# Both ends of a sixteen-head attention pipeline reordered, with a split key row, a later x load and fewer filler matmuls

## The chip, the core and the metric

The kernel runs on one core of a Trainium2 chip. The metric is the device time of that core in microseconds, lower is better. TensorE (PE) multiplies, VectorE (DVE) and ScalarE (ACT) empty the accumulator banks, GpSimd (POOL) does small vector work and indirect DMAs, SyncE (SP) issues most of the loads and stores. The engines run separate instruction streams, which meet only at semaphores.

## The reference, cut to what matters

Four layers of a decoder, each a gated cross attention on a context and a gated feed-forward block, on x of 8 batches x 256 tokens x 256 features. The context has 120 rows for each batch. Every block reads the layer norm of x.

```python
x = x + tanh(g[0]) * attn0(ln(x), ctx)   # one head of 256, key mask
x = x + tanh(f[0]) * moe0(ln(x))         # 8 experts pick 256 tokens each, plus a shared one
x = x + tanh(g[1]) * attn1(ln(x), ctx)   # 16 heads of 16, key bias and mask
x = x + tanh(f[1]) * fourier(ln(x))      # one 256 x 256 matrix after folding
x = x + tanh(g[2]) * attn2(ln(x), ctx)   # 16 heads of 16, key mask
x = x + tanh(f[2]) * ternary(ln(x))      # 256 -> 1024 -> gelu, layer norm -> 256
x = x + tanh(g[3]) * attn3(ctx, ctx, ln(x))  # one head of 256
x = x + tanh(f[3]) * moe3(ln(x))         # top-1 routing, 8 experts of 256 slots
```

Softmax of a one-head attention adds one number for each key to the scores (the mask and the bias terms folded through the weights): the *key row*, 960 numbers for the 8 batches.

## The kernel before

The order on each engine is written out by hand, and one function for each small job stands on each engine with matching semaphores.

**Start.** The two weight matrices of the one-head attention are turned (`turn_weights`), copied by ACT and multiplied (`product`), so that keys come straight from the context. `column` makes two bias columns, `key_row` multiplies one of them (`wkb`) with the context, ACT's `take_row` and a DVE instruction make `krow` of it. `fill(bank, n)` issues n matmuls of ones whose result nobody reads. Each appears in the trace as two instructions. There are fills of 15, 4 and 12 around this work.

**The one-head layers** (`one_gate(L)`, L = 0 and 3) run over 8 batches k. In step s PE turns the normalised rows (`turn_z`), turns the probabilities of the batch before (`turn_p`), makes keys and values of the next (`keys_values`), the scores (`scores`), and for the batch two back the router's turn and logits (`gate_turn`, `logits`) after the product with the values. `scores` first adds the key row to all rows by a float32 matmul with one row of ones. DVE takes the maximum (L1647), ACT the exponential (L1360). For L = 3 the router also finds a slot for each token (`pick_expert`, `group_ranks`, `find_slots` in four groups), POOL moves each of the 16 tiles of rows to its slots by an indirect DMA (`move`), and SP loads the sorted rows `G3` back (L400) for the experts. `FILL` and `fill` calls pad PE here; the last two are 40 before the moves have landed and 22 after.

**The sixteen-head pipeline** (`stream`) runs over 16 units v = 8 batches x layers 1 and 2 in steps s = 0 to 17. Unit v has its scores in step v, turned scores, exponentials and half of its product with the values in step v + 1, and the rest, the normalising and the output product in step v + 2; side work (the Fourier block, and the layer norm of the ternary block) follows in steps from 3 on. Accumulator bank 6 is shared by turned z, queries, keys, values and the side turns; each of them waits for the copy out of the one before it. Banks 0 to 3 hold the scores, 4 and 5 the product with the values, 7 the maxima and outputs. `browT` holds the additive key rows of layers 1 and 2 as three bfloat16 parts, for three rows of ones in `scores`. `tern_rows` makes, ahead of the first step, a row of weights (banks 4 and 5) and two rows of sums (bank 7) for the ternary block. After the last step come 16 tiles of the ternary block (`tern_hidden`, `tern_turn`, `tern_out` on PE; `gelu`, `take_high` on ACT; `tern_stats` L2081, `tern_low` L2088, `tern_add` on DVE; `weigh` L561 on POOL).

Of the kernel before, what the change touches and what calls it, by code (L numbers as in the profile page):

```python
# [5 lines left out]
ALU = mybir.AluOpType  # L6
# [7 lines left out]
P = 128  # L14
# [14 lines left out]
FILL = {0: {0: 6}, 3: {5: 8, 6: 14, 7: 18}}  # L29
# [27 lines left out]
def flamingo_kernel(nc, d, out):  # L57
    ctx = ExitStack()
    with ctx:
# [141 lines left out]

        c.at = 18906
# [73 lines left out]
        UN = 2 * NB  # L276
        one = sems("one", f"{ln_names} K_ps KT_sb V_sb s_ps nmax p_sb pT_ps pT_sb y_ps x")
# [14 lines left out]
        def _(sp):  # L292
# [3 lines left out]
            sp.dma_start(W["v0"][:, :, :], d["Wv0"]).then_inc(load["values"], 16)  # L296
            sp.dma_start(x[:, 4:, :], d["x"][:, 4:, :]).then_inc(load["x"], 16)
# [111 lines left out]
        def _(g):  # L409
# [130 lines left out]
            def stream():  # L540
# [75 lines left out]
        def _(pe):  # L616
# [40 lines left out]
            fill(psum[7], 15)  # L657
# [32 lines left out]
            def one_gate(L):  # L690
# [26 lines left out]
                def scores(k):  # L717
                    pe.wait_ge(q["KT_sb"], b0 + k + 1)
                    pe.wait_ge(q["zT_sb"], b0 + k + 1)
                    if k >= 1:  # L720
                        pe.wait_ge(q["p_sb"], b0 + k)
                    else:
                        pe.wait_ge(su["krow"], 1 + L // 3)
                    o = psum[3][:, 0:TB * SK].rearrange("p (t n) -> p t n", t=TB)
                    mm(o, onesf[0:1, :], bcast(krow[0:1, k * SK:(k + 1) * SK], 1, TB), True, False)
# [49 lines left out]
                def group_ranks(n):  # L775
# [5 lines left out]
                    if n == 3:  # L781
                        fill(psum[3], 12)
# [8 lines left out]
                def main():  # L791
                    pe.wait_ge(su["B_sb"], 1 if L == 0 else 3)
                    if L == 0:
                        fill(psum[7], 12)
# [32 lines left out]
                    else:  # L827
# [3 lines left out]
                        fill(psum[3], 22)  # L831
# [167 lines left out]
            pe.wait_ge(su["col_sb"], 2)  # L999
# [5 lines left out]
            def stream():  # L1005
# [5 lines left out]
                def turn_z(v):  # L1011
# [3 lines left out]
                    else:  # L1015
                        pe.wait_ge(q["V_sb"], max(v, 1))
# [17 lines left out]
                def keys(v):  # L1034
                    L, k = layer(v)
                    if 1 <= v < 5:
                        pe.wait_ge(q["q_sb"], v + 1)
# [4 lines left out]
                    for m_ in range(KC):  # L1042
                        for c in range(KC):
                            m = mm(psum[6][:, m_ * SK:(m_ + 1) * SK], W[f"k{L}"][:, c, m_ * P:(m_ + 1) * P],
# [3 lines left out]
                def values(v):  # L1048
# [7 lines left out]
                    for c in range(KC):  # L1056
                        m = mm(psum[6][0:SK, 0:D], ctxT[:, c, k * SK:(k + 1) * SK], W[f"v{L}"][:, c, :], c == 0, c == KC - 1)
# [1175 lines left out]
```

## Time and profile before

| what | value |
|---|---|
| median of three runs | 892.33 us (891.32 to 895.99) |
| the profiled execution | 897.07 us, its span 895.3 us |
| PE matmul busy | 855.6 us, 96% |
| DVE, ACT, POOL busy | 461.7, 326.6, 210.3 us |
| mean granted TensorE clock | 0.987 |

The profile shows one execution. Times of instructions are microseconds from the start of the span. A group's row gives the start of its first instruction, the time to the end of its last, engine, source line, operation and tiles, and in brackets the idle time before it with what ended it. PEld is the weight load of TensorE. Matmuls are pipelined, so that a PE that is busy all the time need not be at its peak. The 1.8 us between 897.07 and 895.3 lie outside the span.

### The profile page before, as it was taken

To read this page: it belongs to the slowest core of one execution; us is meant where nothing else is said; L and a number is where in the kernel's file an instruction comes from. 1 tells how busy PE (TensorE), PEld (TensorE's weight loads), DVE (VectorE), ACT (ScalarE), POOL (GpSimd) and SP (SyncE) were. 2 spreads that over 40 slices of the span, in tenths; PEclk is the share of its full clock that TensorE was granted. 3 is DMA by queue.
4 is the path that set the end of the run, shared out by engine and by line. 5 is a ranking of instruction groups with operands and counts; after the bars stand their busy time and mean duration, and the time that the engine had idled before them with its cause. 6 is when DMAs were issued, how large, how long until landed. Compare 5 with 4: busy or idle time off the path is not lost.

```text
span 895.3 us, 15721 instructions
## 1 busy us (share of the span) xinstructions
PE 855.6 (96%) x6100; PEld 669.5 (75%) x6108; DVE 461.7 (52%) x1240; ACT 326.6 (36%) x628; POOL 210.3 (23%) x241
## 2 busy tenths in 40 slices
PE   8999999999999998889999999988999999999997
PEld 7776665678888876667777777755777779988886
DVE  2773676500132306577777777766998786000000
ACT  2434122112322222555555645646554441112121
POOL 1121233020434310000100101114665116112212
PEclk9997999999999999899999999999999999999999
DMA  7031911014746338000000000000000012336451
GB/s 238 25 130 36 303 76 50 25 53 165 231 156 198 112 95 300 1 2 1 2 2 1 2 1 1 2 1 1 2 1 2 30 42 91 125 115 201 146 167 22
DMA packets 33877, 70.64 MB, mean 79 GB/s; under 512 B 9218, under 2 KB 23946, under 8 KB 28939
## 3 DMA queue, kind: packets, MB, share of 16 engines
q1 hardware_dynamic: 26937, 59.92, 18.8%
q0 software_dynamic: 6144, 8.31, 4.8%
q10 hardware_dynamic: 722, 1.39, 0.4%
q8 instruction: 49, 0.80, 0.4%
q14 instruction: 25, 0.20, 0.1%
HBM read 54.98 MB, written 14.80 MB: 78 GB/s over the span
## 4 chain that ended last, share of the span: by engine, by line
PE 88%; DVE 6%; ACT 3%; issue 2%; DVEq 1%; POOL 0%; POOLq 0%; ACTq 0%
PE banks L618 80%; DVE small L2018 2%; PE banks L1127 2%; PE banks L1206 1%; ACT arena L1308 1%; PE banks L954 1%; PE banks L1141 1%; ACT arena L1360 1%; PE banks L714 1%; PE banks L1020 1%; ACT arena L1489 1%; PE banks L1165 1%; ACT arena L1504 0%; DVE arena L2058 0%; DVE small L1647 0%
## 5 line engine op out<-in xcount | busy, mean ns | idle before, releaser
L618 PE MATMUL banks<-arena 32*120 32x256 f32 (+6 forms) x1808 | 160.1, 378 | 7.2 <-DVE small L2018 4.2
L1308 ACT ACTIVATE arena<-banks 128x512 f32<-128x512 f32 (+4 forms) x185 | 106.8, 597 | 163.1 <-PE banks L1091 34.3
L618 PEld LDWEIGHTS banks<-arena 32*120 32x120 f32 (+5 forms) x1808 | 99.6, 164 | 38.4 <-issue 19.0
L618 PE MATMUL banks<-ffw,arena 128*128 128x256 bf16 (+2 forms) x632 | 116.7, 338 | 0.5 <-issue 0.2
L618 PE MATMUL banks<-arena,ew 128*128 128x256 f32 x512 | 113.3, 379 | 1.4 <-ACT arena L1308 1.4
L618 PE MATMUL banks<-ew,arena 128*128 128x256 f32 x512 | 113.2, 379 | 0.0
L618 PEld LDWEIGHTS banks<-arena,ew 128*128 128x128 f32 x512 | 97.1, 190 | 15.0 <-ACT arena L1308 1.8
L618 PEld LDWEIGHTS banks<-ew,arena 128*128 128x128 f32 x512 | 96.2, 190 | 12.5
L618 PEld LDWEIGHTS banks<-ffw,arena 128*128 128x128 f16 (+1 forms) x640 | 84.5, 135 | 23.8 <-issue 2.4
L2018 DVE TENSOR_REDUCE small<-banks 128x16 f32<-128x1920 f32 x32 | 69.1, 2158 | 23.6 <-PE banks L618 23.6
L1965 DVE TENSOR_SCALAR arena<-banks,arena 128x256 f32<-128x256 f32 x16 | 7.1, 479 | 120.7 <-PE banks L618 120.7
L1504 ACT ACTIVATE arena<-banks,mcol 120x2048 f32<-120x2048 f32 x32 | 63.2, 1974 | 16.6 <-PE banks L618 16.6
L545 POOL TENSOR_TENSOR small<-small,mhalf 128x2 f32<-128x2 f32 x16 | 11.1, 694 | 210.9 <-DVE small L1989 210.9
L618 PE MATMUL banks<-arena,ffw 128*128 128x512 f32 x128 | 60.4, 615 | 0.0
L1445 ACT ACTIVATE arena<-banks,b1T 128x256 f32<-128x256 f32 x64 | 26.9, 471 | 77.8 <-PE banks L618 77.8
L1942 DVE TENSOR_SCALAR small<-arena,tg 128x2 f32<-128x2 f32 x8 | 1.8, 228 | 97.0 <-PE banks L618 97.0
L1447 ACT ACTIVATE arena<-banks 128x256 f32<-128x256 f32 x64 | 21.1, 381 | 83.2 <-PE banks L618 83.2
L1338 ACT ACTIVATE arena<-banks,b1T 128x512 f32<-128x512 f32 x32 | 21.9, 687 | 76.9 <-PE banks L618 76.9
L430 POOL TENSOR_TENSOR small<-small,mhalf 128x2 f32<-128x2 f32 x31 | 22.6, 730 | 107.4 <-DVE small L1624 107.4
L506 POOL DMA_INDIRECT out<-arena x14 | 21.8, 1557 | 92.5 <-DVE arena L1965 64.8
L516 POOL DMA_INDIRECT arena<-zrow,small x16 | 17.9, 1116 | 103.4 <-DVE arena L1947 57.0
L618 PEld LDWEIGHTS banks<-arena,ffw 128*128 128x128 f32 x128 | 23.4, 195 | 23.1 <-issue 22.6
(244 smaller groups left out, 1309.8 us busy)
## 6 DMA issues: line engine op xcount, KB each, us to landing
ew<-in_w SPq DMA_DIRECT2D x32, 1024.0 KB, 7.2
xrow<-arena SPq DMA_DIRECT2D x1, 2064.0 KB, 20.9
arena<-xrow SPq DMA_DIRECT2D x8, 258.0 KB, 4.3
zrow<-arena SPq DMA_DIRECT2D x8, 256.0 KB, 2.2
ffw<-in_shared SPq DMA_DIRECT2D x2, 1024.0 KB, 6.4
acc<-x SPq DMA_DIRECT2D x4, 512.0 KB, 3.5
ffw<-in_tern SPq DMA_DIRECT2D x2, 1024.0 KB, 8.2
out<-x SPq DMA_DIRECT2D x8, 256.0 KB, 2.0
```

Source lines behind the costliest of these rows:

```text
L430: g.tensor_tensor(rstd[:, 2 * a:2 * a + 2], ve[:, 2 * a:2 * a + 2], mhalf[:, 0:2], ALU.pow).then_inc(q["rstd"], 1)
L506: g.indirect_dma_start(to, bass.IndirectOffsetOnAxis(ap=at(e, j), axis=0), eout[:, e % 2, j, :], None, compute_op=ALU.add, **kw).then_inc( ...
L516: g.indirect_dma_start(G[:, u, j, 0:ROW], None, zrow, bass.IndirectOffsetOnAxis(ap=idx[:, TB * e + j:TB * e + j + 1], axis=0))\
L545: g.tensor_tensor(rstd[:, 2 * u:2 * u + 2], ve[:, 2 * u:2 * u + 2], mhalf[:, 0:2], ALU.pow)\
L618: return pe.matmul(o, l, r, start=a, stop=b)
L1127: m = pe.transpose(OW[:, 512 * t + g_ * P:512 * t + (g_ + 1) * P], OP[:, g_, t * P:(t + 1) * P], ident[:, :])
L1308: return nc.scalar.activation(o, i_, ACT.Copy)
L1338: nc.scalar.activation(hT[:, m_, :], psum[m_ % 4][:, :], ACT.Gelu_apprx_tanh, bias=b1T[:, E * MC + m_:E * MC + m_ + 1]).then_inc(sh["h_sb" ...
L1445: m = nc.scalar.activation(heT[:, u, m_, :], src, ACT.Gelu_apprx_tanh, bias=b1T[:, n * MC + m_:n * MC + m_ + 1])
L1447: m = nc.scalar.activation(heT[:, u, m_, :], src, ACT.Relu)
L1504: nc.scalar.activation(PT[0:SK, c].rearrange("p h n -> p (h n)"), SC[0:SK, :], ACT.Exp, bias=mcol[0:SK, L - 1, k:k + 1]).then_inc(q["p_exp ...
L2018: V.tensor_reduce(nmx[:, t, :], s, AX.X, ALU.max, negate=True).then_inc(q["max"], 1)
```

## The change

1. **Start.** The fills are 8, 2 and none (from 15, 4, 12). The column for `wkb` is made first, in bank 7, and handed over with a semaphore of its own. ACT issues the context's load after the two tiny ones, and SP issues the rest of x only when the context has landed.
2. **First steps of the stream.** `tern_rows` is split in three, put between `keys(0)`, `values(0)`, `turn_z(0)` and `queries(0)`. DVE normalises batch 0 ahead of `take_values(0)`. Unit 1 has its keys and values in bank 5; in step 0 its keys come ahead of the second half of the scores and its queries behind it, and its values are made in step 1. ACT and DVE take them in the same order.
3. **Steps 2 and 3** issue `output(s - 2)` ahead of `values(s + 1)`.
4. **End of the stream.** `side_norm(14)` moves from step 17 to behind `tern_stats(2)`; `tern_stats(0)` goes ahead of the last `add_output`, `tern_low(0)` ahead of `tern_stats(1)`.
5. **Key row of layer 3.** POOL splits `krow` into three bfloat16 parts in steps 8 to 10 (`key_part`), SP copies each into a row of `browT`, and `scores` of L = 3 uses one bfloat16 matmul with three rows of ones.
6. **Fills in layer 3**: `FILL` 8, 14, 18 becomes 6, 14, 15; 12 becomes 9 in `group_ranks`; 22 becomes 5 after the moves.

```diff
-FILL = {0: {0: 6}, 3: {5: 8, 6: 14, 7: 18}}
+FILL = {0: {0: 6}, 3: {5: 6, 6: 14, 7: 15}}
...
+        def kv(v):
+            return 5 if v == 1 else 6
...
             sp.dma_start(W["v0"][:, :, :], d["Wv0"]).then_inc(load["values"], 16)
+            sp.wait_ge(load["ctx"], 16)
             sp.dma_start(x[:, 4:, :], d["x"][:, 4:, :]).then_inc(load["x"], 16)
...
+            for p in range(3):
+                sp.wait_ge(su["parts"], p + 2)
+                sp.dma_start(browT[p:p + 1, 0, :], kpart[0:1, :]).then_inc(load["parts"], 16)
...
+                def key_part(p):
+                    if p == 0:
+                        g.wait_ge(su["krow"], 2)
+                        g.wait_ge(multi["s_ps"], 2 * NB)
+                    else:
+                        g.wait_ge(load["parts"], 16 * (p + 1))
+                    g.tensor_copy(kpart[0:1, :], krow[0:1, :])
+                    g.drain().then_inc(su["parts"], 1)
+                    if p < 2:
+                        g.tensor_tensor(krow[0:1, :], krow[0:1, :], kpart[0:1, :], ALU.subtract)
+                        g.drain()
...
+                    if NB <= s < NB + 3:
+                        key_part(s - NB)
+                    elif s == NB + 3:
+                        g.wait_ge(load["parts"], 16 * 4)
...
-            fill(psum[7], 15)
+            fill(psum[7], 8)
...
-            fill(psum[7], 4)
+            fill(psum[7], 2)
             pe.wait_ge(su["wT_sb"], 2)
             pe.wait_ge(load["cols"], 16)
+            column(psum[7][:, 0:KC], WT[:, 1], COL["q0"]).then_inc(su["col_ps"], 1)
             product(psum[4], WT[:, 1], WT[:, 0]).then_inc(su["B_ps"], 1)
             column(psum[5][:, 0:KC], WT[:, 0], COL["k0"])
-            column(psum[5][:, KC:2 * KC], WT[:, 1], COL["q0"])
...
-                    mm(o, onesf[0:1, :], bcast(krow[0:1, k * SK:(k + 1) * SK], 1, TB), True, False)
+                    if L == 0:
+                        mm(o, onesf[0:1, :], bcast(krow[0:1, k * SK:(k + 1) * SK], 1, TB), True, False)
+                    else:
+                        mm(o, ones[0:3, :], bcast(browT[0:3, 0, k * SK:(k + 1) * SK], 1, TB), True, False)
...
-                        fill(psum[3], 12)
+                        fill(psum[3], 9)
...
                     if L == 0:
-                        fill(psum[7], 12)
                         pe.wait_ge(load["values"], 32)
...
                         fill(psum[3], 40)
                         pe.wait_ge(gt["moved"], 16 * NT)
-                        fill(psum[3], 22)
+                        fill(psum[3], 5)
...
                 keys(0)
+                tern_weights()
                 values(0)
-                tern_rows()
+                tern_row(0)
                 turn_z(0)
+                tern_row(1).then_inc(su["trow_ps"], 1)
...
+                    if s == 1:
+                        values(1)
                     if past:
                         attend(s - 2, 1)
-                    if free and new:
+                    if new and (free or s == 0):
                         keys(s + 1)
...
                     if now:
                         scores(s, 1)
-                    if spectrum:
+                    if spectrum or s == 0:
                         queries(s + 1)
...
-                    if new:
+                    if past and not free:
+                        output(s - 2)
+                    if new and s:
                         values(s + 1)
-                    if past:
+                    if free:
                         output(s - 2)
...
             act.dma_start(cols[:, :], d["cols"]).then_inc(load["cols"], 16)
-            act.dma_start(ctxT[:, :, :], d["ctxT"]).then_inc(load["ctx"], 16)
             act.dma_start(tg[:, :], d["g"].partition_broadcast(P)).then_inc(load["tiny"], 16)
             act.dma_start(m0_i[0:1, :], d["m0"]).then_inc(load["tiny"], 16)
+            act.dma_start(ctxT[:, :, :], d["ctxT"]).then_inc(load["ctx"], 16)
...
                         first_stats()
+                        v.wait_ge(su["col_ps"], 1)
+                        V.tensor_copy(wkb, psum[7][:, 0:KC]).then_inc(su["col_sb"], 1)
                         first_rows()
-                        v.wait_ge(su["col_ps"], 1)
-                        V.tensor_copy(wkb, psum[5][:, KC:2 * KC])
+                        v.wait_ge(su["col_ps"], 2)
...
+                v.wait_ge(load["x0"], 32)
+                norm_batch(0)
+                norm_batch_end(0)
                 take_values(0)
-                v.wait_ge(load["x0"], 32)
-                for n in range(2):
-                    norm_batch(n)
-                    norm_batch_end(n)
+                norm_batch(1)
+                norm_batch_end(1)
...
-                    if s >= 3:
+                    if 3 <= s <= UN:
                         side_norm(s - 3)
-                    if s + 1 < UN:
+                    if 1 <= s < UN - 1:
                         take_values(s + 1)
+                    if s == UN + 1:
+                        tern_stats(0)
                     if s >= 2:
                         add_output(s - 2)
-                tern_stats(0)
+                tern_low(0)
                 tern_stats(1)
-                tern_low(0)
+                tern_low(1)
                 tern_stats(2)
-                tern_low(1)
+                side_norm(UN - 2)
```

## Rows read from the trace of the kernel before

**Rows 1.** The page's part 4: the chain that ended last, by engine.

```profile
PE 88%; DVE 6%; ACT 3%; issue 2%; DVEq 1%; POOL 0%; POOLq 0%; ACTq 0%
```

**Rows 2.** Windows: length, busy time (instructions) of PE, PEld, DVE, ACT, POOL, PEclk, DMA share, GB/s.

```profile
1.40:4.40 3.00, 2.98 (x14) 2.98 (x15) 0.00 (x0) 0.66 (x1) 0.28 (x1) 1.00 0.73 214
...
66.00:68.00 2.00, 2.00 (x7) 1.40 (x8) 0.75 (x3) 0.00 (x0) 0.69 (x1) 0.50 0.00 0
...
356.00:360.00 4.00, 2.81 (x26) 1.78 (x22) 3.02 (x6) 2.27 (x3) 0.00 (x0) 0.50 0.00 0
```

**Rows 3.** Timeline of the start.

```profile
1.42 4.96 PE L618 MATMUL banks<-onesf 128*128 128x128 f32 x30 [1.42 <-POOLq L414]
...
3.34 0.37 ACTq L1326 DMA_DIRECT2D rows<-in_rows  x1
...
5.21 0.37 DVE L1780 TENSOR_REDUCE small<-ident 128x16 f32<-128x128 f32 x1 [5.21 <-DMA ident<-in_ident]
...
6.23 0.60 PE L630 MATMUL banks<-ident,Wq 128*128 128x128 f32 x4
...
12.31 0.99 PE L618 MATMUL banks<-ctxT,small 128*1 128x240 f32 x16 [0.47 <-DVE cols L1722]
...
13.23 2.94 PE L618 MATMUL banks<-onesf 128*128 128x128 f32 x24
...
23.13 0.74 DVE L1619 BATCH_NORM_STATS2 small<-x 128x6 f32<-128x256 f32 x2
```

**Rows 4.** DMA issues of the first 30 us: queue, KB each, microseconds to landing.

```profile
x<-in_x SPq DMA_DIRECT2D x1, 1536.0 KB, 12.1
ctxT<-in_ctxT ACTq DMA_DIRECT2D x1, 960.0 KB, 7.2
...
rows<-in_rows ACTq DMA_DIRECT2D x1, 128.0 KB, 11.6
```

**Rows 5.** Timeline of the stream's first steps.

```profile
338.17 3.66 PE L618 MATMUL banks<-ffw,small 128*128 128x256 bf16 x32
...
345.94 0.38 PE L618 MATMUL banks<-browT,ones 3*128 3x480 bf16 x4 [0.93 <-ACT arena L1478]
...
356.93 2.16 DVE L2018 TENSOR_REDUCE small<-banks 128x16 f32<-128x1920 f32 x1 [0.81 <-PE banks L618]
...
368.96 1.97 ACT L1504 ACTIVATE arena<-banks,mcol 120x2048 f32<-120x2048 f32 x1 [1.09 <-PE banks L618]
```

**Rows 6.** Timeline of step 2: the values of unit 3.

```profile
384.64 1.12 PE L618 MATMUL banks<-Wv,ctxT 128*120 128x256 f32 x4 [0.77 <-ACT arena L1489]
```

**Rows 7.** Timeline of the stream's last step and the first ternary tiles.

```profile
616.55 4.00 POOL L561 TENSOR_TENSOR arena<-arena 128x1024 f32<-128x1024 f32 x2 [1.02 <-ACT arena L1531]
616.77 3.93 DVE L2058 TENSOR_SCALAR arena<-x,small,arena 128x256 f32<-128x256 f32 x2
...
624.98 1.16 PE L1206 MATMUL banks<-ident,arena 128*128 128x128 f32 x8 [1.79 <-DVE arena L2088]
```

**Rows 8.** Timeline of layer 3, step 3: the key row and the scores.

```profile
717.78 0.67 PE L618 MATMUL banks<-krow,onesf 1*128 1x240 f32 x2
...
718.38 1.15 PE L618 MATMUL banks<-arena 128*128 128x120 f32 x8
```

**Rows 9.** The chain in order of time, layer 3: start, length, what.

```profile
709.09 3.45 PE banks L618 x22
...
716.10 3.45 PE banks L618 x22
```

**Rows 10.** Timeline from the last router work to the first expert.

```profile
759.57 14.09 PE L618 MATMUL banks<-onesf 128*128 128x128 f32 x124
...
767.30 3.97 SPq L400 DMA_DIRECT2D arena<-xrow  x8
773.39 0.47 PEld L954 LDWEIGHTS banks<-ident,arena 128*128 128x128 f32 x4
```

**Rows 11.** The line L400: the loads of the sorted rows.

```profile
DMA to landing us min/median/max: 2.8/4.3/5.1
```

More of the change, by code:

```diff
@@ L200, in flamingo_kernel @@
         digit = c.take(2 * P, "p (a t e) -> p a t e", dt=F16, a=2, e=E)
+        c.at = 15360
+        kpart = c.take(NB * SK, dt=BF16)
         c.at = 18906
@@ L721, in scores @@
                         pe.wait_ge(q["p_sb"], b0 + k)
+                    elif L == 0:
+                        pe.wait_ge(su["krow"], 1)
                     else:
-                        pe.wait_ge(su["krow"], 1 + L // 3)
+                        pe.wait_ge(load["parts"], 16 * 4)
                     o = psum[3][:, 0:TB * SK].rearrange("p (t n) -> p t n", t=TB)
-                    mm(o, onesf[0:1, :], bcast(krow[0:1, k * SK:(k + 1) * SK], 1, TB), True, False)
+                    if L == 0:
+                        mm(o, onesf[0:1, :], bcast(krow[0:1, k * SK:(k + 1) * SK], 1, TB), True, False)
+                    else:
+                        mm(o, ones[0:3, :], bcast(browT[0:3, 0, k * SK:(k + 1) * SK], 1, TB), True, False)
                     for t in range(TB):
@@ L998, in _ @@
             pe.wait_ge(su["B_sb"], 3)
-            pe.wait_ge(su["col_sb"], 2)
+            pe.wait_ge(su["col_sb"], 3)
             pe.wait_ge(sh["x"], T // 512 * 2 + 1)
@@ L1182, in tern_rows, with tern_row @@
                            ident[:, :], True, True)
-                    for a in range(2):
-                        for m_ in range(MC):
-                            for l in range(2):
-                                m = mm(psum[7][:, a * D:(a + 1) * D], lnhl[:, l, a, m_:m_ + 1].to_broadcast([P, P]), wp[:, m_, :],
-                                       m_ == 0 and l == 0, m_ == MC - 1 and l == 1)
-                    m.then_inc(su["trow_ps"], 1)
+                def tern_row(a):
+                    for m_ in range(MC):
+                        for l in range(2):
+                            m = mm(psum[7][:, a * D:(a + 1) * D], lnhl[:, l, a, m_:m_ + 1].to_broadcast([P, P]), wp[:, m_, :],
+                                   m_ == 0 and l == 0, m_ == MC - 1 and l == 1)
+                    return m
                 def tern_hidden(t):
@@ L1248, in stream @@
                         turned_scores(s - 1, 0)
-                    if new and not free:
+                    if 1 <= s < 4:
                         queries(s + 1)
@@ L1488, in take_keys @@
                         for e in range(2):
-                            m = nc.scalar.activation(KB[:, v % 3, c, e], psum[6][:, c * SK:(c + 1) * SK], ACT.Identity,
+                            m = nc.scalar.activation(KB[:, v % 3, c, e], psum[kv(v)][:, c * SK:(c + 1) * SK], ACT.Identity,
                                                      bias=kb[:, L - 1, c, e:e + 1], scale=par[:, e:e + 1])
@@ L1542, in stream @@
                 act.wait_ge(ex["y_sb"], E)
-                for part in (take_keys, take_z, take_queries):
-                    part(0)
+                take_keys(0)
+                take_z(0)
                 act.wait_ge(su["trow_ps"], 1)
@@ L1547, in stream @@
                     copy(wrow[:, 512 * j:512 * (j + 1)], psum[4 + j])
+                take_queries(0)
                 for s in range(UN + 2):
@@ L1558, in stream @@
                         take_O(s - 2)
-                    if free and new:
+                    if new and (free or s == 0):
                         take_keys(s + 1)
@@ L1573, in stream @@
                         take_back(s - 2)
-                    if new and not free:
+                    if 1 <= s < 4:
                         take_keys(s + 1)
@@ L2103, in stream @@
                         maxima(s, 0)
+                    if s == 1:
+                        take_values(1)
                     if s >= UN - 1:
```

18 lines of the change are left out of this document (9 added, 9 removed).

## The prediction

> **What bounds the kernel now.** I read the chain that ended last first: TensorE carries 88% of it [rows 1]. So what counts is TensorE's idle time, the work that it does for nothing, and its clock. The windows show the clock twice at 0.50, its 1.2 GHz level, in a stage with regular short waits and in the first steps of the stream [rows 2]. Then I read the timelines of the places that the edits touch and looked, for each, at what TensorE waits for last. In the middle of the stream and in the experts it is busy without pause; no edit touches these. The sum is made against the profiled execution's 897.07 us; the median of the runs shown, 892.33, is 4.7 below it, and the forecast is taken from the median.
>
> **1. Start.** The 15 fills end at 1.42 + 4.96 = 6.38, and the transposes begin at 6.23, overlapping their tail [rows 3]. The identity that they need has landed at 5.21, and Wq stands ahead of it in the same queue [rows 3]. The first 14 fill instructions take 3.0 us, 0.213 each [rows 2], the later fills 2.94 / 24 = 0.12 [rows 3]. So 8 fills (16 instructions) end near 4.7, and the transposes start at 5.3: 0.9 gained. From there to the key row it is 6.1 us of work, in which the order of the columns changes nothing in sum; the 4 fills that become 2 lie under ACT's copy. The key row waited 0.47 for DVE's column [rows 3]; that column is now ready first, 0.47 gained. The key row ends at 13.3 and 12 fills follow up to 16.17 [rows 3]; without them the first keys could start at 12.0 where they started at 16.0. They also need the value row of 128 KB, issued last in ACT's queue at 3.34 and landed 11.6 later, at 14.9 [rows 3, 4]. That row shared the DMA with the 1536 KB of x, which took 12.1 us [rows 4]. Now x starts only when the context is in. The context took 7.2 us; issued 1.1 later with less beside it I put it, and the row behind it, at 9 to 10.5. So the term is 4.0, of which I take **3.8**. Its lower end is 1.0 (the row still lands at 14.9), its upper end 4.2. SP's queue behind its new wait holds the rest of x and fourteen further loads; the first to be missed is x. It is wanted by DVE for the third batch at 23.13 [rows 3], now 19.3. Loaded from 9.5 with a share of the queue, it comes at 15 to 17; if it takes 12.1 as before, it comes 2.3 late, and that is the price of that cover.
>
> **2. First steps of the stream.** Before, TensorE does the weight row and then 3.66 us of sums [rows 5] in one piece, after it turns z, waits for ACT's copy, and makes the queries. Now the weight row (some 1.7) fills the wait for the first key copy, and the second half of the sums (1.8) covers ACT's copy of z (1.2 with its wait). DVE and the reload of x give back about 1: the normalised batch 0 is wanted 3 us earlier than before and is not ready. Net 1.7: the first scores move from 345.94 [rows 5] to 344.3. In step 0 the queries of unit 1 (2.0) no longer stand between the first maximum and the second half of the scores, which waited 1.0 too long for them: 2.7. The next scores waited for a chain of queries, keys, copy (1.5) and values (1.1); the keys now come early in their own bank and the values later, so what is left is the queries and their copy: 3.4 to 3.7, and DVE's maximum of unit 1 moves from 356.93 [rows 5] to 353.2. From there on the work of step 1 ran at clock 0.50 [rows 2]: the turned scores took about 1.1 longer than in the next pair, the maxima waited with them. With TensorE fed more densely I take the clock as kept, 1.3 more: the exponential of 368.96 [rows 5] comes at 364.0. Term **5.0**, lower end 3.5 (the clock falls here all the same), upper end 5.7. ACT's copies of the weight row (1.1) now precede the query copy; they are covered by the queries' own 2.0.
>
> **3. Steps 2 and 3.** TensorE waits 0.77 for ACT's key copy before the values [rows 6], while the output product, whose input is ready, stands behind. Swapped, it fills that wait: 0.77 in each of two steps, **1.5**. Lower end 0 (ACT's exponential, which ends about 0.2 before the next scores can start, becomes the bound), upper end 1.6.
>
> **4. End of the stream.** DVE's two normalising instructions take 3.93 us, from 616.77 to 620.70, exactly under POOL's pair of 4.00 [rows 7]; elsewhere in the stream such a pair takes 0.73. All of DVE's work behind them is late: the copies that TensorE's second tile turn waits 1.79 for, until 624.98 [rows 7]. With `side_norm(14)` moved and the low part of tile 0 first, that low part is there at 622.9. TensorE then goes on when its own hidden product ends, at 623.0: 2.0 gained. Moved behind the third tile's statistics, `side_norm(14)` (0.73, or up to 2.0 more under the next POOL instruction) makes the first `tern_add` late, for which TensorE's second output product waits: 0.4 lost. Term **1.6**, from 0.5 to 2.2.
>
> **5. Key row in three parts.** The float32 key row starts at 717.78 and the scores behind it at 718.38 [rows 8]: 0.60. The nearest row for the new form is the stream's: four bfloat16 matmuls of 480 columns in 0.38 [rows 5], with the next matmul some 0.2 after their start. So one of 240 columns is 0.2, and 0.4 is saved in each batch. The chain runs through this block with period 7.01 (716.10 - 709.09) [rows 9]. DVE has 0.8 idle in such a step, so it does not stop a saving of 0.4. From the router's first group on (steps 6 and 7) DVE has no idle time, and nothing is gained. Six batches, **2.4**, from 1.0 to 3.0. The price is five POOL instructions on one partition and three DMAs, in three steps of the stream in which POOL is idle for most of the time. Queued behind them on POOL is the side layer norm's power, wanted by DVE some 5 us later. A POOL instruction of 1024 columns took 2.0 [rows 7], so copy and subtraction cost up to 4.0 of these 5: nothing.
>
> **6. Fills of layer 3.** The fills of 8 and 18 in the router steps end about when their input is there, so 2 and 3 fewer gain 0.4 once. After the router 124 instructions run in 14.09 [rows 10], 0.114 each: 40 fills end at 768.7, the last 22 at 773.5, and then the first expert turns its rows at 773.39. These rows are issued at 767.30 [rows 10] and land 2.8 to 5.1 later [rows 11], the first of them, I take it, with the least: 770.1. With 5 fills TensorE is free at 769.8. Term 3.2 with the start of the fills unchanged against the moves, taken as **3.0**; if the first load lands with the median, 4.3, it is 1.8. The moves themselves start with the router's slots, which move with term 5.
>
> **Sum.** 3.8 + 5.0 + 1.5 + 1.6 + 2.4 + 3.0 = 17.3. Against the profiled execution 897.07 - 17.3 = 879.8; from the median 892.33 - 17.3 = **875.0**. The lower ends add to 7.8 (884.5), the upper ends (3.3 for the last) to 20.0 (872.3).
>
> **The clock weighed.** The profiled execution has two stretches at 0.50 and is 4.7 above the median, so I price a further stretch at 3 to 5. Removed fills leave TensorE idle for 0.6 at the start and 0.3 before the experts. The Trainium skill, in TensorE: Matmul & The Clock Gate, section HAM oscillation, has TensorE fall back to half rate when it idles and return only after sustained work, which speaks against removing fills. By it the start would run slow again; by the rows TensorE is past its slow level from about 4.4 us on, and the idle stretches are far shorter than the regular waits of a layer-0 step, which it ran through at 1.00 for 40 us.
>
> **The rivals.**
> - *The clock falls once more than before*, at the start (6.1 us of work at 0.213 to 0.12: up to 4.5 lost) or in layer 3 with its thinner fills. For it: regular short waits did bring it down at 66 [rows 2]. Against it: 105 of the 151 fills stay. 875.0 + 4.5 = 879.5. Chance 0.17.
> - *Gains that other waits take over*: the value row lands late (2.8 less), the first sorted rows with the median (1.2), the key row is hidden under DVE (2.4). 875.0 + 6.4 = 881.4. Chance 0.14.
> - *POOL's split stalls DVE.* Rows 7 show two DVE instructions held for as long as POOL's run. Five instructions of up to 2.0 in steps 8 to 10 could hold DVE 10 us; about half of it would reach TensorE, which is busy all through these steps: 880. The Trainium skill, SBUF — State Buffer, section Who interferes with whom, makes this an exclusive lock between GpSimd and a DVE instruction of this kind; the trace agrees with its 3.93 beside 4.00. Chance 0.05.
> - *The clock does not fall in layer 0 either*, since its steps are 3.8 earlier: 871. Chance 0.07.
> - *Slower: POOL holds up the side chain.* `key_part` waits on POOL for the DMA of the part before; the side power is behind it, then DVE's side work, then TensorE's side turn in bank 6. It decides when copy, landing and subtraction take over 10 us in each of steps 8 to 11: 17.3 are used up by 4.4 lost in each, and 5.7 lost makes 898. Against it: small loads of the sorted rows landed in 2.8 [rows 11]. Chance 0.03.
> - *It does nothing that can be measured*: 890. Chance 0.03.
>
> **Numbers.** The forecast itself has 0.51, with a range of its own of 871.5 to 878.5. 868 to 884 takes in the first five cases. A measurement of this kernel tells 0.5%, 4.5 us, from no change. Faster 0.94, within it 0.03, slower 0.03.
>
> **What would show it.** Right: the transposes at 5.3, the first keys near 12, no clock of 0.50 between 340 and 365, the exponential of unit 0's second half 4.9 nearer to the stream's first keys, no DVE pair of 3.9 at the end, a layer-3 period of 6.6, and the first expert 2.8 to 3.2 after the sorted rows' issue. Wrong: first keys at 15, steps 8 to 10 longer than the 17.05 of their neighbours, or a new stretch at 0.50 in a place with fewer fills.

## The result, and the profile after

| | kernel before | changed kernel |
|---|---|---|
| beside each other, four executions each | 892.3 us (891.32 to 895.99) | 881.28 us (881.06 to 882.34) |
| the profiled execution | 897.07 us | 881.06 us, its span 879.3 us |
| on another chip, 11 and 5 executions | 899.21 us (896.45 to 903.04) | 883.55 us (882.79 to 884.82) |

The ratio is 0.9864, 95% interval 0.9832 to 0.9897; on the second chip 0.983, 0.9805 to 0.9855. So the change makes the kernel faster, inside the wide range of the forecast (868 to 884) but outside the forecast's own 871.5 to 878.5: by 11.0 us between the medians where 17.3 were forecast. On the second chip the medians differ by 15.7, profile against profile it is 16.0.

The same instructions in the two traces show where it comes from. Each pair is the start of one instruction, in microseconds:

| landmark | before | after | gained so far |
|---|---|---|---|
| first weight turns | 6.23 | 4.99 | 1.24 |
| key row of layer 0 | 12.31 | 10.93 | 1.38 |
| first keys of layer 0 | 16.01 | 11.84 | 4.17 |
| first keys of the stream | 332.75 | 323.15 | 9.60 |
| exponential of unit 0's second half | 368.96 | 353.49 | 15.47 |
| second ternary tile's turn | 624.98 | 606.12 | 18.86 |
| side turn of unit 14 | 636.42 | 621.43 | 14.99 |
| a key row of layer 3, early | 703.25 | 687.47 | 15.78 |
| the next one | 710.77 | 696.62 | 14.15 |
| the fills of 40 | 759.57 | 743.61 | 15.96 |
| issue of the sorted rows | 767.30 | 753.05 | 14.25 |
| first expert of layer 3 | 773.39 | 755.87 | 17.52 |
| end of the span | 895.3 | 879.3 | 16.0 |

Four gains are given back: 3.9 us behind the second ternary turn, 1.6 between two key rows, 1.7 between the fills of 40 and the issue of the sorted rows, 1.5 in the first expert. The start, in the timeline, answers to [rows 3]:

```profile
1.42 3.78 PE L646 MATMUL banks<-onesf 128*128 128x128 f32 x16 [1.42 <-POOLq L425]
...
3.18 0.45 ACTq L1365 DMA_DIRECT2D rows<-in_rows  x1
4.99 1.06 PE L658 MATMUL banks<-ident,Wq 128*128 128x128 f32 x4
...
10.89 0.33 SPq L305 DMA_DIRECT2D x<-in_x  x1
10.93 0.98 PE L646 MATMUL banks<-ctxT,small 128*1 128x240 f32 x16
...
11.84 1.15 PE L646 MATMUL banks<-ctxT,Wq 128*128 128x120 f32 x8
```

And the loads of the first 30 us (KB each, microseconds to landing), which answer to [rows 4]:

```profile
x<-in_x SPq DMA_DIRECT2D x1, 1536.0 KB, 7.7
ctxT<-in_ctxT ACTq DMA_DIRECT2D x1, 960.0 KB, 8.1
...
rows<-in_rows ACTq DMA_DIRECT2D x1, 128.0 KB, 8.0
```

The value row lands at 3.18 + 8.0 = 11.2 instead of 14.9, ahead of the first keys. The rest of x lands at 18.6, and VectorE, which needs it for batch 2, takes it up at 19.07 without a wait. The 1.14 that TensorE waits at 18.87 are for batch 1, whose rows are in the early part of x: VectorE normalises them behind the first maximum. The kernel before has the same wait, 1.15 at 22.94. The stream's first steps, which answer to [rows 5]:

```profile
323.15 1.05 PE L646 MATMUL banks<-ctxT,Wk 128*128 128x120 f32 x8
...
333.64 0.38 PE L646 MATMUL banks<-browT,ones 3*128 3x480 bf16 x4 [0.93 <-ACT arena L1517]
...
353.49 1.97 ACT L1543 ACTIVATE arena<-banks,mcol 120x2048 f32<-120x2048 f32 x1 [1.09 <-PE banks L646]
```

The windows (columns as in [rows 2]): the two stretches of before, and three places where the clock is low now:

```profile
66.00:68.00 2.00, 1.53 (x9) 1.20 (x9) 1.20 (x6) 0.38 (x1) 0.48 (x1) 1.00 0.00 0
356.00:360.00 4.00, 3.29 (x55) 2.16 (x54) 2.98 (x5) 2.00 (x3) 0.00 (x0) 1.00 0.00 0
614.00:618.00 4.00, 4.00 (x21) 2.58 (x20) 2.94 (x8) 0.00 (x0) 0.79 (x2) 0.62 0.00 0
692.00:696.00 4.00, 4.00 (x22) 3.97 (x22) 3.54 (x14) 0.87 (x2) 1.23 (x2) 0.57 0.17 66
757.00:760.00 3.00, 2.79 (x7) 2.25 (x8) 0.00 (x0) 0.16 (x1) 0.00 (x0) 0.50 1.04 340
```

The old ones are at 1.00; the new ones are short, 3.4 us each at 0.50, the 1.2 GHz level: 10.2 us in all, where the kernel before had 13.65 and 6.8, each beside a last one at the end of the span. Now the ternary block's first tiles, which answer to [rows 7]:

```profile
604.78 1.29 DVE L2129 TENSOR_TENSOR arena<-banks,arena 128x512 f16<-128x512 f32 x2 [0.31 <-ACT arena L1347]
606.12 1.04 PE L1239 MATMUL banks<-ident,arena 128*128 128x128 f32 x8
...
610.12 0.71 DVE L2099 TENSOR_SCALAR arena<-x,small,arena 128x256 f32<-128x256 f32 x2
...
611.34 2.00 POOL L572 TENSOR_TENSOR arena<-arena 128x1024 f32<-128x1024 f32 x1
611.42 2.20 DVE L1652 SCALAR_TENSOR_TENSOR x<-arena,small,x 128x256 f32<-128x256 f32 x1
613.76 5.21 PE L646 MATMUL banks<-ffw,arena 128*128 128x256 bf16 x24 [2.26 <-DVE x L1652]
```

The pair of 3.93 under POOL is gone and the second tile turn follows at once. But `side_norm(14)` (L2099) now stands ahead of `tern_add(0)` (L1652), which starts 0.08 behind POOL's next instruction, takes 2.20 where the next one takes 0.48, and TensorE waits 2.26 for it. Then the clock falls, and 24 matmuls that take 3.64 a tile earlier take 5.21.

Layer 3 and its end, which answer to [rows 8] and [rows 10]:

```profile
703.24 0.27 PE L646 MATMUL banks<-browT,ones 3*128 3x240 bf16 x1
...
703.44 1.15 PE L646 MATMUL banks<-arena 128*128 128x120 f32 x8
...
749.13 0.96 POOL L433 DMA_INDIRECT xrow<-arena,small  x1 [0.30 <-issue]
753.05 4.00 SPq L411 DMA_DIRECT2D arena<-xrow  x8
753.08 1.38 PE L646 MATMUL banks<-onesf 128*128 128x128 f32 x10 [0.29 <-DMA xrow<-arena,small]
755.87 0.65 PE L986 MATMUL banks<-ident,arena 128*128 128x128 f32 x4 [1.41 <-DMA arena<-xrow]
```

The scores start 0.20 behind the key row instead of 0.60. The first expert starts 2.82 behind the issue of its rows; in this execution it waits for them and no longer for fills.

### The profile page after: what moved, and what is told of

Read it like the earlier page. It is cut to its first block and busy times, and to the rows that moved or that the text cites. A ratio compares the mean times of both kernels' runs of the same rounds, so it can differ in the third digit from the quotient of the medians.

```text
span 879.3 us, 15545 instructions
## 1 busy us (share of the span) xinstructions
PE 840.4 (96%) x6008; PEld 656.6 (75%) x6008; DVE 460.9 (52%) x1240; ACT 326.5 (37%) x628; POOL 216.8 (25%) x246
## 5 line engine op out<-in xcount | busy, mean ns | idle before, releaser
L646 PE MATMUL banks<-arena 32*120 32x256 f32 (+6 forms) x1808 | 155.9, 373 | 7.1 <-DVE small L2059 4.1
L646 PEld LDWEIGHTS banks<-arena 32*120 32x120 f32 (+5 forms) x1808 | 97.3, 161 | 35.8 <-issue 16.0
L646 PE MATMUL banks<-ffw,arena 128*128 128x256 f32 (+2 forms) x640 | 118.8, 342 | 2.3 <-DVE x L1652 2.3
L646 PEld LDWEIGHTS banks<-ew,arena 128*128 128x128 f32 x512 | 96.2, 190 | 12.5
L646 PE MATMUL banks<-arena,ffw 128*128 128x512 f32 x128 | 58.6, 601 | 0.0
```

What stands on the lines that cost most here:

```text
L646: return pe.matmul(o, l, r, start=a, stop=b)
```

## The experiments

All ran beside the kernel before. Since executions of one kernel differ by up to 12.5 us with the granted clock of the whole execution, the ranges are given too.

**One part alone, from the kernel before.** First the kernel before itself.

> The kernel before, unchanged. Theory (the profiled base held a clock stretch of its own): the executions that are not profiled at 896 lack the 0.50 stretch of layer 0, so the median is 891.5 to 892.5, and a profile of such an execution shows layer 0 about 5 us shorter than the 320.7 us from first keys to the stream's first keys seen before. Rival (the stretch is in every execution of this kernel): this profile shows it again, at about 66 to 79 us, whatever the time.

899.09 us (895.6 to 906.36, 32 executions); the 12 of the second copy 898.62, ratio 0.9987 (0.9955 to 1.0019). An execution's time follows its clock: 895.6 to 896.9 at a granted 0.996, 895.7 to 899.4 at 0.995 to 0.993, 904.4 to 904.7 at 0.984. The profile is of one of 904.63:

```profile
68.00:82.00 14.00, 13.01 (x40) 9.26 (x39) 7.71 (x30) 2.53 (x8) 1.83 (x3) 0.53 0.12 39
```

So the long stretch of layer 0 is not a trait of one profile: it came again in a long execution, and so did the one in the stream's first steps, with a further one of 3.4 us from 14.3 on. From the first keys to the stream's first keys both profiles take 316.7 to 316.8 us (the 320.7 of the expectation is a slip). The executions at 0.996 can't hold it, since 13.7 us at half rate alone take 0.008 off a mean. The forecast of its median missed, since on this chip the kernel is 7 us slower (last section); that the base held a stretch which other executions lack holds.

```diff
# the start alone
-            fill(psum[7], 15)
+            fill(psum[7], 8)
+            sp.wait_ge(load["ctx"], 16)
...
# the stream's first steps alone
+            return 5 if v == 1 else 6
...
# the key row alone
+                        mm(o, ones[0:3, :], bcast(browT[0:3, 0, k * SK:(k + 1) * SK], 1, TB), True, False)
```

> The kernel before with only the start changed (fills, the column ahead of the product, x's rest and the context reordered). Theory (the trace's 4.17 us at the first keys is kept to the end, and layer 0's clock stretch belongs to one execution): median about 4 us below the kernel before, 888. Rival A (the start decides where layer 0's clock falls): up to 9.6 us less, 883. Rival B (layer 0 takes the gain back in another wait): 0 to 1 us less, 891.

892.69 us (889.95 to 897.86), ratio 0.9928 (0.9894 to 0.9962): 6.4 less. In the trace the gain is 4.29 us at the first keys and 4.19 behind them, of which a fall of the clock at 19 us takes 1.66. Layer 0's stretch is there, but 3.4 us long where it was 13.65. So the 4.2 are kept, and the clock adds its part, here and in the stream, where the stretch of before is absent too.

> The kernel before with only the first steps of the two-batch stream changed (order of keys, values, queries and TernaryLN's row turns, unit 1 in bank 5). Prediction's terms 2 and 3: 5.0 + 1.5 us, so 885.8; the two traces put 5.87 + 1.43 = 7.3 us there, 885.0. Rival (a short clock fall elsewhere gives part of it back): 887 to 889, and the profile shows a stretch at 0.50 that the kernel before has not.

893.61 us (890.18 to 900.95), ratio 0.9939 (0.9905 to 0.9972): 5.5 less. From the stream's first keys to step 4 the trace gains 7.3 us, of which 1.85 stand for the stretch at 356 to 363 us. That stretch is absent as well in the profiles with the start alone and with the key row alone, whose streams are those of before:

```profile
348.00:356.00 8.00, 6.14 (x80) 4.53 (x78) 4.69 (x10) 5.02 (x6) 0.69 (x1) 1.00 0.01 2
```

(start alone, whose stream begins 7.07 earlier). The new order itself gives 5.45. Of the four profiles with the old order two have the stretch, of the ten with the new order none; whether the order keeps it away is not shown.

> The kernel before with only layer 3's key row in three parts. Prediction's term: 2.4 us, so 889.9; period of the gate 6.61 instead of 7.01 us. Rival A (the keys no longer keep the clock, or POOL's parts delay the stream): 0 to 1 us less. Rival B (the whole of the period counts for all eight units and the sorted rows too): 3 us less.

898.93 us (894.59 to 907.07), ratio 1.0014 (0.9976 to 1.0052): no gain that shows. Period and scores are as forecast, and steps 8 to 10 keep their length; but its profile has new stretches at 702 to 705 and 756 to 763 us. Rival A holds in this profile by its clock half, not by POOL. The wait of TensorE in front of the first gate turn is 1.10 us here, and 0.69 in the kernel before: the 0.4 that the key row saves in this step become idle time, and the first of the two stretches follows 2.5 us behind it.

**The changed kernel and its undone parts.**

> The changed kernel, unchanged, beside the kernel before on another chip. Theory (the change saves 15 to 16 us of work and waits, and what the medians show depends on which clock stretches each execution falls into): ratio between 0.982 and 0.986, and every execution's time follows its granted clock. Rival (the last moves of layer 3's gate wait 4 to 7 us longer on this chip, as in the four profiles before, and the changed kernel does not): ratio near 0.978. Rival (the profiled 16 us were the base's bad execution): 0.988.

883.55 us (882.79 to 884.82), ratio 0.983 (0.9805 to 0.9855): the first theory's place. Its second half misses: the execution with the lowest clock, 0.988, took 883.36, the three at 0.991 took 883.55 to 884.82. The first rival's wait is there, in both kernels (last section).

```diff
# normalization later
                 tern_stats(2)
-                side_norm(UN - 2)
...
-                    if t == 4:
+                    if t == 3:
+                        side_norm(UN - 2)
+                    elif t == 4:
```

> The changed kernel with unit 14's normalization for the spectral layer behind the third tern_low instead of ahead of the first tern_add. Theory (that place pushed tern_add(0) under POOL's weigh(3): 2.20 us instead of 0.48, then 2.26 us of PE idle and a 0.50 stretch at 614 us): 3.5 us below the changed kernel, tern_add(0) back at about 0.5 us, no stretch at 614. Rival (the stretch comes whatever the order, since TernaryLN's first tiles are thin): at most 1.7 us less, stretch still there. Rival (unit 14's side turn is now late): 0.

879.09 us (878.53 to 881.14), ratio 0.9783 (0.9757 to 0.9808), 4.5 below the changed kernel on the same chip; the executions of the two do not overlap. Landmarks move by 3.8 us between 610 and 625 and nowhere else before 690. The timeline and the window:

```profile
610.88 0.48 DVE L1652 SCALAR_TENSOR_TENSOR x<-arena,small,x 128x256 f32<-128x256 f32 x1
...
611.48 2.00 POOL L572 TENSOR_TENSOR arena<-arena 128x1024 f32<-128x1024 f32 x1
611.51 3.63 PE L646 MATMUL banks<-ffw,arena 128*128 128x256 bf16 x24
...
614.00:618.00 4.00, 4.00 (x34) 3.23 (x33) 3.85 (x10) 2.18 (x4) 2.53 (x3) 1.00 0.01 4
```

`tern_add(0)` is done 0.12 before POOL starts, TensorE does not wait, and the clock stays. One call of 0.7 us of VectorE work in the wrong place costs 3.8.

```diff
# end of the stream as before
-                    if 3 <= s <= UN:
+                    if s >= 3:
                         side_norm(s - 3)
...
-                tern_low(0)
+                tern_stats(0)
                 tern_stats(1)
-                tern_low(1)
+                tern_low(0)
                 tern_stats(2)
-                side_norm(UN - 2)
+                tern_low(1)
```

> The changed kernel with the end of the stream in the order of before (statistics and low parts of TernaryLN's first tiles, and unit 14's normalization). Prediction's term 4: 1.6 us above the changed kernel. Theory: the two traces lost 1.9 us in this part, so 1.9 us below it, with no stretch at 614.

882.71 us (881.26 to 890.48), ratio 0.9831 (0.9795 to 0.9867); the three executions with granted clock 0.995 are at 881.3 to 881.6. In its trace this part is 1.9 us shorter than in the changed kernel, with no stretch at 614. The medians differ by 0.8 only, with overlapping intervals. So in the traces the part as changed is a loss of 1.9, and with its one call moved a gain of 1.9.

```diff
# layer 3's fills as before
-FILL = {0: {0: 6}, 3: {5: 6, 6: 14, 7: 15}}
+FILL = {0: {0: 6}, 3: {5: 8, 6: 14, 7: 18}}
...
-                        fill(psum[3], 9)
+                        fill(psum[3], 12)
...
-                        fill(psum[3], 5)
+                        fill(psum[3], 22)
```

> The changed kernel with layer 3's fills as before (8, 14, 18; 12; 22). Prediction's term 6: 3.0 us above the changed kernel (first expert later by 17 fills of 0.11 us and the rest). Theory: the short count let the clock fall at 757 us, which costs the first expert 1.55 us, so that only 1.3 to 1.5 us above it, and no stretch at 757. Rival: the stretch stays although the fills are back: 3 us above.

891.3 us (884.44 to 891.63), ratio 0.9901 (0.987 to 0.9933). The two executions at 0.992 and 0.994 took 886.5 and 884.4; four at 0.986 or 0.987 took 891.2 to 891.6, and none of these is profiled. In the profile of 886.51 the first expert starts 1.7 us later, though a fall at 693 that costs 1.6 is missing in it: 3.3 for the fills. TensorE is at fills until the expert's start at 762.75, 8.9 behind the issue of the rows. The theory's saving is not seen: the clock was at 0.50 during the fills, not in the expert. The third line of the expectation, 3 us, fits the profile; the further 5 to 7 us of most executions fit none. Their clock is lower by 0.005 to 0.008, and 13.65 us at half rate, the stretch that layer 0 has in other profiles, take 0.0077 off a mean: an explanation that no profile of them shows. The first expert has no stretch in this profile, and none in the changed kernel's second profile either (there 747.6 to 754.4, at the ranks and fills): the one at 757 stands in one profile only.

```diff
# the key row as before, in the kernel with the later normalization
-                        mm(o, ones[0:3, :], bcast(browT[0:3, 0, k * SK:(k + 1) * SK], 1, TB), True, False)
+                    mm(o, onesf[0:1, :], bcast(krow[0:1, k * SK:(k + 1) * SK], 1, TB), True, False)
```

> The kernel with the later normalization (ratio 0.9783 to the kernel before) and layer 3's key row again one fp32 row. Prediction's term 5: 2.4 us above it, ratio 0.981; period of the gate 7.01 us again. Rival (the bf16 key row is what lets the clock fall at 689 us, so undoing it gives 1.4 us back): ratio 0.9795, no stretch between 685 and 700 us. Rival (as in the kernel with the key row alone, whose ratio was 1.0014): no difference, 0.978.

881.87 us (881.06 to 886.91), ratio 0.981 (0.9771 to 0.9849), 2.8 above the kernel with the later normalization. The chain in order of time has the period of 7.01 again:

```profile
697.34 3.44 PE banks L637 x22
704.35 3.44 PE banks L637 x22
711.36 3.44 PE banks L637 x22
```

The intervals overlap; the lowest executions, 881.06 and 878.53, differ by 2.5. In this company the key row is worth what was forecast, as far as six and five executions tell. The first rival's sign is there all the same: no stretch between 685 and 700 us. With the float32 row TensorE waits 0.69 in front of the first gate turn, with the bfloat16 row 1.09:

```profile
693.94 0.66 PE L779 MATMUL banks<-ident,arena 128*128 128x128 f32 x4 [0.69 <-DVE arena L1660]
```

```profile
689.91 0.66 PE L793 MATMUL banks<-ident,arena 128*128 128x128 f32 x4 [1.09 <-DVE arena L1674]
```

(this kernel, then the changed kernel). Over all profiles: behind the 0.69 the clock fell in none of five, behind the 1.09 in five of seven. The profiles with fills as before and with the end of the stream as before have the 1.09 and no fall.

```diff
# fitted fills, in the kernel with the later normalization
-FILL = {0: {0: 6}, 3: {5: 6, 6: 14, 7: 15}}
+FILL = {0: {0: 6}, 3: {0: 4, 5: 6, 6: 14, 7: 15}}
...
-                        fill(psum[3], 40)
+                        fill(psum[3], 28)
```

> The kernel with the later normalization, four fills in front of layer 3's first gate turn (into 1.09 us of TensorE idle) and 28 fills instead of 40 behind the last ranks. Theory: no 0.50 stretch at 689 (1.4 us back), and the first expert no longer waits for fills that outlast the moved rows: 1 to 2.3 us there; together 2 to 3.5 us, ratio 0.9745 to 0.976. Rival (fewer fills let the clock fall in the first expert): 1.5 us lost there, net 0 to 1 us gained. Rival (four fills make the gate's first turns late): 0.9 us lost at 689.

877.4 us (876.92 to 883.6), ratio 0.9766 (0.9726 to 0.9807), the lowest ratio of all. The medians differ by 1.7, less than the 2 to 3.5 expected, with overlapping intervals; the profiles differ by 3.4. Landmarks gain 1.64 at 689 and 1.72 at the first expert. The four fills in their wait, and the window with the clock, here and then in the kernel with the later normalization:

```profile
685.11 1.06 PE L646 MATMUL banks<-onesf 128*128 128x128 f32 x8
686.37 0.66 PE L793 MATMUL banks<-ident,arena 128*128 128x128 f32 x4 [0.19 <-DVE arena L1674]
...
688.00:692.00 4.00, 4.00 (x30) 3.48 (x31) 3.54 (x14) 1.32 (x4) 0.77 (x2) 1.00 0.17 66
```

```profile
688.00:692.00 4.00, 4.00 (x23) 4.00 (x24) 3.54 (x15) 0.87 (x2) 0.91 (x2) 0.58 0.17 66
```

Between these two profiles, four fills, some 0.9 us in a wait of 1.09, stand for a fall worth 1.6. That they prevent it is not shown: with them no profile of two has it, without them five of seven have it and two do not. At the end TensorE is free again before the rows are there: the first expert starts 2.98 behind their issue, where the kernel with 40 fills took 5.07.

```diff
# without the fills ahead of the late gate turns and the last ranks
-FILL = {0: {0: 6}, 3: {5: 6, 6: 14, 7: 15}}
+FILL = {0: {0: 6}, 3: {}}
...
-                    if n == 3:
-                        fill(psum[3], 9)
```

> The kernel with the later normalization, without the fills ahead of layer 3's late gate turns (6, 14, 15) and ahead of the last ranks (9). Theory A (the pause of TensorE behind the last ranks, 3 to 5 us on these chips, comes from the dense fills and their instructions): VectorE's wait for remote falls from 4.4 to 5.1 us to under 1, the last two moves are issued 3 to 4 us earlier. Theory B (it has another cause): the pause stays, and the thinner stretch lets the clock fall earlier, 0 to 2 us slower.

879.47 us (877.61 to 881.48), ratio 0.9773 (0.9737 to 0.9809), the same as with them. Theory B: the wait stays (4.23), and the clock is low throughout:

```profile
723.00:747.00 24.00, 15.21 (x98) 13.43 (x96) 11.85 (x57) 3.13 (x11) 14.86 (x16) 0.50 0.27 94
```

The clock is low for 24 us, and the nearly equal median hides what it costs. The timelines of this kernel and of the one with the fills, issue of the sorted rows and first expert:

```profile
753.64 3.99 SPq L411 DMA_DIRECT2D arena<-xrow  x8
756.61 0.66 PE L984 MATMUL banks<-ident,arena 128*128 128x128 f32 x4 [0.76 <-DMA arena<-xrow]
```

```profile
751.58 4.78 SPq L411 DMA_DIRECT2D arena<-xrow  x8
756.65 0.60 PE L986 MATMUL banks<-ident,arena 128*128 128x128 f32 x4
```

The rows are issued 2.1 us later, and the first expert is not, only because with the fills it had stood behind the 40 fills until 756.65. So the 44 fills are worth up to 2 us, by one pair of profiles, where nothing else covers them.

```diff
# fills at the start, in the kernel with the fitted fills
+                        if L == 0 and s == 1:
+                            fill(psum[7], 5)
```

> The kernel with the fitted fills (ratio 0.9766 to the kernel before, 876.9 to 877.8 us in five executions and 883.6 us in one) and five fills in layer 0's second step, into the 1.14 us in which TensorE waits for x's rest. Theory (the executions that are some 6 us longer are those whose clock falls at 19 us and then for 13.65 us at 63, as three profiles of it showed): all executions below 879 us, median unchanged at 877.4, PE idle before the second turns under 0.3 us. Rival (the falls have another cause): some executions at 883 to 885 us again. Rival (the fills make the second turns late): 0.2 to 0.5 us more.

878.14 us (876.88 to 881.3), ratio 0.9772 (0.9745 to 0.98). The wait of 1.14 is filled and the second turns are not late (landmarks move by 0.1). It was the wait for batch 1's normalised rows, not for x's rest as the expectation has it, and of the three profiles with a fall at 19 us two have 13.65 us at half rate behind it and one 3.4. No execution is at 883 or above, but one is at 881.3, and five are too few for an event that 1 in 6 had. Inconclusive.

## Why the prediction was right, and where its sizes were off

Direction and wide range were right; the forecast gain is 6.3 us too large against the medians, 1.6 on the second chip. The measured 881.28 stands next to the 881.4 of the rival *gains that other waits take over*, but none of its three parts came: the value row landed in time, the first sorted rows were there 2.82 behind their issue, and the key row's 0.4 was seen where it was forecast, if not in every step. The range holds by terms that offset each other, which is luck in part.

**1. Start** (3.8): right, 4.17, in both kernels that have it. The transposes came at 4.99 (5.3 forecast), the keys at 11.84 (12.0), x's rest at 18.6 where 15 to 17 was taken, and still before VectorE wanted it at 19.07 (19.3 forecast). In the steps behind the gain is 4.07.

**2. and 3. The stream's first steps** (5.0 and 1.5): 5.87 and 1.43 between the traces. Without the 1.85 of the stretch at 356, which two kernels with the old order lack as well, the two terms are 5.45 in sum, where 5.2 of the forecast 6.5 were for the order and 1.3 for the clock. Whether the clock's part belongs to the edit is open.

**4. End of the stream** (1.6): the term that failed. The first half was right to a tenth, 1.96 at the second tile turn. The prediction itself named the second half, that `side_norm(14)` "makes the first `tern_add` late", and priced it at 0.4. It measured 3.9: `tern_add` was not only late but pushed under POOL's next instruction (2.26 of wait), and the clock fell with the wait (1.57). The prediction had the 2.0 of such a meeting in its hands from [rows 7] but applied it to `side_norm` and not to its successor. The Trainium skill, SBUF — State Buffer, section Who interferes with whom, says that a VectorE instruction with two SBUF inputs contends with a GpSimd instruction that reads SBUF; `tern_add` adds two SBUF tiles, and the trace agrees: 2.20 beside 2.00 of POOL, 0.48 without.

**5. Key row** (2.4): size right: between the two profiles 0.40 in each of five steps (0.60 to 0.20), 2.0 in all, and 2.5 to 2.8 when undone in the faster kernel. Alone it gained nothing in the medians; in its one profile the clock fell twice more. What the prediction did not see is the step of the first gate turn: there the saving became TensorE's idle time, 1.09 instead of 0.69, and in five of seven profiles the clock fell behind it, for 1.6. The term never asked what a shorter key row does to the clock.

**6. Fills** (3.0): the time from the rows' issue to the first expert shrank from 6.09 to 2.82, 3.27, as forecast. On the second chip it is 5.18, at fills again. The issue itself gave back 1.3 in this execution (3.92 from the last move to it, 2.44 to 2.84 in the thirteen other profiles), and a fall in the first expert 1.5. The prediction had 0.3 of idle time before the expert; TensorE waited 0.29 and then 1.41.

**The clock** was the rival of chance 0.17, "at the start or in layer 3 with its thinner fills", and it came twice in layer 3 at 1.6 and 1.5, once at the stream's end. The Trainium skill, TensorE: Matmul & The Clock Gate, section HAM oscillation, speaks of idling as the cause. The traces agree in part: the fall is in five of seven profiles with the wait of 1.09 in front of it and in none of seven with 0.69 or 0.2, and without the fills of the rank stage the clock stayed low for 24 us; but two profiles have the 1.09 and no fall, so that the wait alone does not decide it.

**The base.** The profiled execution of before was 4.7 us above the median, and layer 0's 13.65 us at half rate are of that size: two profiles of kernels with the same layer 0 and a stretch of only 3.4 us are 4.5 to 4.6 us shorter from layer 0's first keys to the stream's. No other execution of that chip is profiled, so this fits and is not shown. The rival by which the clock does not fall in layer 0 came true in the profile, where layer 0 is 5.4 us shorter, and not in the 871 that was put on it, since it was subtracted from a median that may hold little of the stretch. So the forecast subtracted from the median terms read in an execution that was longer for another reason; these terms were its own, but the 16.0 between profiles is 11.5 without the 4.5. Sum of what is left over: 17.3 forecast, less 3.5 for term 4, less 3.1 for two falls, gives 10.7; measured 11.0. That it comes so near is chance in part: the other deviations, the 1.3 of the issue among them, cancel, and on the second chip, where the changed kernel has the same falls at 614 and 693, the medians differ by 15.7.

What makes layer 0's stretch 0, 3.4 or 13.7 us long is not settled. In 14 profiles the four with the old start had one always. The ten with the new start had none in seven; in the other three the clock had fallen at 19 us first, behind the wait of 1.14 for batch 1's rows, which six of the seven have as well.

## What to carry to other kernels

- When an instruction is moved, look at what its successor now runs beside, not only at how late it is: 0.7 us of VectorE work cost 3.8 by pushing a two-input add under GpSimd.
- Here fills were worth something only in idle time of a stage that TensorE bounds. Four in a wait of 1.09 stood for 1.6 between two profiles; 22 instead of 5 (and 8 more ahead) in front of the first expert cost 3.3 in a third.
- A shorter instruction in front of a wait makes the wait longer. The key row's 0.4 became idle time in one step, and in five of seven profiles the clock fell behind it.
- Before a gain is summed, compare the profiled execution's granted clock with those of the others. A stretch at half rate that executions of one kernel have or lack can't be credited to an edit from one pair of profiles.

## What the runs showed that was not expected

In all twelve later profiles, on three chips, VectorE waits 4.2 to 5.2 us at the last ranks of layer 3, in the first two profiles 1.07 and 0.65. TensorE's matmuls that it needs are recorded as done at once; the profile names no instruction that ended the wait ("remote"), and TensorE's fills behind them have gaps with no wait. From the second profile of the changed kernel:

```profile
746.36 0.58 PE L646 MATMUL banks<-onesf 128*128 128x128 f32 x3
747.27 0.59 PE L646 MATMUL banks<-onesf 128*128 128x128 f32 x3 [0.33 <-issue]
748.69 1.23 PE L646 MATMUL banks<-onesf 128*128 128x128 f32 x5 [0.83 <-issue]
...
750.31 0.17 DVE L1729 TENSOR_SCALAR arena<-banks 128x16 f32<-128x16 f32 x1 [4.42 <-remote]
```

From layer 3's last key row to the end of the span, the kernel before takes 4.5 us more in its second profile than in its first, the changed one 3.1 more; falls of the clock have a part in this. The medians of the later chips are 6.9 us higher for the kernel before and 2.3 for the changed one, and why the two differ so is not explained. VectorE's wait stays without the fills, so they are not the cause. What is, and why the first two profiles have only 1.07 and 0.65, stays open.
